# Two adapters and a mix on one Trainium2 core: the tile pipeline in two phases, and the mix as three products

## What is computed

```python
x = ...                       # 64 sequences x 32 rows x 512 features, fp32; the rows of one sequence share indices
# first block: a gated MLP, F = 1376, each of the three matrices with a rank-16 adapter chosen per sequence (16 adapters)
gate = x @ W_gate.T + 0.5 * (x @ A_gate[i].T) @ B_gate[i].T
up   = x @ W_up.T   + 0.5 * (x @ A_up[i].T)   @ B_up[i].T
act  = silu(gate) * up
h    = x + act @ W_down.T + 0.5 * (act @ A_down[i].T) @ B_down[i].T
# second block: the 32 rows of a sequence are mixed by one of 16 matrices of 32 x 32
out  = h + einsum('bct,bcd->bdt', h, weights[j])
```

## Time and profile before

| | us |
|---|---|
| three executions, median (lowest, highest) | 507.98 (503.09, 508.24) |
| the profiled execution, its own time | 507.72 |
| its span (first to last instruction) | 505.9 |
| PE busy in it | 480.2 (95%) |
| DVE / ACT / POOL busy | 237.8 / 159.4 / 118.6 |

### The profile page before, as it was taken

One profiled execution on the slowest core, in us unless ns is written; L12 is line 12 of the kernel. 1 busy time (PEld: TensorE's weight loads), 2 busy tenths in 40 slices (PEclk: granted clock), 3 DMA queues, 4 the chain that ended last, 5 costly groups with the idle time before them and its releaser, 6 DMA issues.

```text
span 505.9 us, 7251 instructions
## 1 busy us (share of the span) xinstructions
PE 480.2 (95%) x2716; PEld 430.2 (85%) x2716; DVE 237.8 (47%) x447; ACT 159.4 (32%) x244; POOL 118.6 (23%) x166
## 2 busy tenths in 40 slices
PE   2798599999999999999999999999999999999996
PEld 2677489899898989989898998989899898989985
DVE  2786525436353543635354362535536262553622
ACT  2764314232231424224142412414241241424120
POOL 5006040402305040220505022050502205050100
PEclk9799889999999999999999999999999999999998
DMA  7886151240604225060512406051240705123010
GB/s 246 325 263 228 60 200 48 64 180 1 223 21 171 73 74 171 1 223 21 171 73 78 167 1 224 19 183 62 87 157 2 230 12 195 50 92 132 1 41 21
DMA packets 16725, 58.13 MB, mean 115 GB/s; under 512 B 3184, under 2 KB 3696, under 8 KB 14672
## 3 DMA queue, kind: packets, MB, share of 16 engines
q0 software_dynamic: 5888, 36.97, 20.6%
q1 hardware_dynamic: 10832, 21.10, 12.9%
HBM read 53.86 MB, written 4.19 MB: 115 GB/s over the span
## 4 chain that ended last, share of the span: by engine, by line
PE 87%; DMA 4%; DVE 3%; POOL 3%; ACT 1%; issue 1%; SPq 0%; POOLq 0%; DVEq 0%
PE ps_down L673 26%; PE ps_gate L641 8%; PE ps_gate L643 8%; PE ps_gate L642 8%; PE ps_up L643 7%; PE ps_up L641 7%; PE ps_up L642 7%; PE ps_turn L662 4%; DMA b_raw<-in_b_rows,rows_now 3%; PE ps_misc L692 3%; POOL a_raw L322 3%; PE ps_gate L651 2%; PE ps_gate L650 2%; PE ps_up L650 2%; PE ps_up L651 2%; PE ps_down L683 2%
## 5 line engine op out<-in xcount | busy, mean ns | idle before, releaser
L446 DVE TENSOR_TENSOR actT_lo<-ps_turn,actT_hi 128x256 fp32r<-128x256 f32 (+1 forms) x64 | 32.0, 521 | 150.1 <-ACT actT_hi L346 115.4
L641 PE MATMUL ps_gate<-w_gate_hi,xT_hi 128*128 128x512 f32 (+3 forms) x196 | 77.8, 397 | 12.8 <-DVE w_gate_lo L446 12.8
L346 ACT ACTIVATE actT_hi<-ps_turn 128x256 fp32r<-128x256 f32 (+1 forms) x64 | 27.9, 461 | 165.6 <-PE ps_turn L662 162.1
L643 PE MATMUL ps_gate<-w_gate_hi,xT_lo 128*128 128x512 f32 (+3 forms) x196 | 77.3, 394 | 0.0
L642 PE MATMUL ps_gate<-w_gate_lo,xT_hi 128*128 128x512 f32 (+3 forms) x196 | 76.8, 392 | 0.0
L673 PE MATMUL ps_down<-wd_hi,actT_hi 128*128 128x288 f32 (+1 forms) x352 | 76.6, 299 | 0.0
L673 PE MATMUL ps_down<-wd_hi,actT_lo 128*128 128x288 f32 (+1 forms) x352 | 75.5, 295 | 0.0
L673 PE MATMUL ps_down<-wd_lo,actT_hi 128*128 128x288 f32 (+1 forms) x352 | 75.5, 296 | 0.0
L641 PE MATMUL ps_up<-w_up_hi,xT_hi 128*128 128x512 f32 (+1 forms) x192 | 74.1, 386 | 0.4 <-DVE w_up_lo L446 0.4
L331 POOL COPY mix_rows_now<-rows 128x1 int32 (+1 forms) x16 | 3.0, 187 | 300.4 <-DVE mix_w L509 300.4
L643 PE MATMUL ps_up<-w_up_hi,xT_lo 128*128 128x512 f32 (+1 forms) x192 | 71.3, 371 | 0.0
(11 more groups left out here) (66 smaller groups left out, 628.7 us busy)
## 6 DMA issues: line engine op xcount, KB each, us to landing
xT_raw<-in_xT SPq DMA_DIRECT2D x16, 256.0 KB, 2.6
x_sb<-in_x SPq DMA_DIRECT2D x16, 256.0 KB
out<-out_sb SPq DMA_DIRECT2D x15, 256.0 KB
landing<-in_w_down SPq DMA_DIRECT2D x5, 512.0 KB, 4.7
landing<-in_w_gate SPq DMA_DIRECT2D x4, 512.0 KB, 5.2
landing<-in_w_up SPq DMA_DIRECT2D x4, 512.0 KB, 4.8
a_raw<-in_a_rows,rows_now POOLq DMA_INDIRECT x64
landing<-in_w_gate SPq DMA_DIRECT2D x2, 352.0 KB, 3.8
```

What stands on the lines that cost most here:

```text
L346: return nc.scalar.activation(dst, src, ACT.Copy)
L446: return nc.vector.tensor_tensor(dst, src, hi_part.bitcast(F32), ALU.subtract)
L641: pe.matmul(ps[:, cols], x_hi, hi, start=(k == 0 and not columns), stop=False)
L643: last = pe.matmul(ps[:, cols], x_lo, hi, start=False, stop=stops and k == KH - 1)
```

## The change

The work is cut into two phases. **Phase 1** runs over 8 pairs of tiles and does gate and up only: six units per pair (three sections by two tiles), three PSUM banks each for gate and up instead of two, B rows gathered per section. A pair's eight sequences are dealt to its two tiles in an interleaved way. The activation isn't turned on PE: DVE transposes it in 32 x 32 blocks into `staging` (L679 of the changed kernel), and SP stores it to a DRAM tensor `actT_dram` that is already turned (`spill`, four DMAs per section and pair). **Phase 2** runs over 16 tiles: load `actT_dram`, split it, 66 down products, down adapter and mix of the tile before. Its POOL code is `gather_down`, its DVE code is the second `down`, its PE code the third. The SBUF of the gate and up weights is reused by the buffers of phase 2. The mix is three fp32r products of 512 columns: `mix_hi`, `mix_lo` by `h_hi`, `h_lo`, whose splitting is new work on ACT and DVE.

The core of the diff:

```diff
+                reached(ve, spilled[s], 64 * pr)
+                ve.wait_ge(act_ready, NU * pr + k + 1)
+                nc.vector.transpose(staging[s][:, :, t, :], act[k % 2][:, 0:n].rearrange("p (j c) -> p j c", c=BLOCK))\
+                    .then_inc(act_turned, 1)
...
+            def spill(pr, s):
+                c0, n = SECTIONS[s]
+                sp.wait_ge(act_turned, NU * pr + 2 * s + 2)
+                for q in range(TILE_SEQS):
+                    at = (q % 2) * 2 * BLOCK
+                    sp.dma_start(
+                        actT_dram[bass.ds(2 * pr + q // 2, 1), c0:c0 + n, at:at + 2 * BLOCK]
+                        .rearrange("o (j f) c -> f (o j) c", f=BLOCK),
+                        staging[s][q * BLOCK:(q + 1) * BLOCK, :, :, :].rearrange("f j t c -> f j (t c)"))\
...
+            def load_actT(m, e):
+                for s in range(NS):
+                    sp.wait_ge(spilled[s], 64 * (m // 2 + 1) if isinstance(m, int) else 64 * PAIRS)
+                reached(sp, actT_ready, m - 1)
+                sp.dma_start(
+                    actT_raw[e][:, 0:(NC - 1) * P].rearrange("p (c n) -> p c n", n=P),
+                    actT_dram[bass.ds(m, 1), 0:(NC - 1) * P, :].rearrange("o (c p) n -> p (o c) n", p=P))\
+                    .then_inc(actT_landed[e], 16)
...
+            def gather_down(m, first=False):
+                at = TILE_SEQS + 1
+                reached(pool, a_dn_ready, m)
+                pool.tensor_copy(a_dn_now[:, :], now(m)[:, at:at + TILE_SEQS]).then_inc(a_dn_now_copied, 1)
+                indirect_after(a_dn_now_copied, m + 1)
+                for q in range(TILE_SEQS):
+                    gather(a_dn_raw[:, q, :], a_dn_rows, a_dn_now[:, q:q + 1]).then_inc(a_dn_landed, 16)
+                reached(pool, mix_ready, m)
+                pool.tensor_copy(mix_now[:, :], now(m)[:, at + TILE_SEQS + 1:COLS]).then_inc(mix_now_copied, 1)
+                indirect_after(mix_now_copied, m + 1)
+                gather(mix_raw[:, :], mix_rows, mix_now[:, :]).then_inc(mix_landed, 16)
+                reached(pool, b_dn_ready, m)
+                pool.tensor_copy(b_dn_now[:, :], now(m)[:, at + TILE_SEQS:at + TILE_SEQS + 1])\
+                    .then_inc(b_dn_now_copied, 1)
+                if first:
+                    pool.wait_ge(xT_used[0], PAIRS)
+                    pool.wait_ge(xT_used[1], PAIRS)
+                indirect_after(b_dn_now_copied, m + 1)
+                gather(b_dn_raw[:, :], b_dn_rows, b_dn_now[:, :]).then_inc(b_dn_landed, 16)
...
-            def gathers(t, first=False):
-                if not first:
-                    pool.wait_ge(a_dn_ready, t)
-                    pool.wait_ge(b_dn_ready, t)
-                now = rows[:, bass.ds(t, 1), :].rearrange("p o c -> p (o c)")
-                pool.tensor_copy(rows_now[:, :], now[:, 0:TILE_SEQS + 1])\
...
+            def split_mix(m):
+                ve.wait_ge(mix_hi_ready, m + 1)
+                for q in range(TILE_SEQS):
+                    r = slice(q * CH, (q + 1) * CH)
+                    last = lo(mix_lo[r, r], mix_raw[r, :], mix_hi[r, r])
+                last.then_inc(mix_ready, 1)
...
+            def down(m, e, first=False, last=False):
+                if not first:
+                    mask_td(m - 1, 1 - e)
+                    split_mix(m - 1)
+                if not last:
+                    split_a_dn(m + 1, 1 - e)
+                if not first:
+                    residual_h(m - 1, 1 - e)
+                if not last:
+                    split_actT(m + 1, 1 - e)
+                split_b_dn(m)
+                if not first:
+                    residual_out(m - 1, 1 - e)
...
+            def pair(pr, final=False):
+                base(pr, 0)
+                lora(pr - 1, 5)
+                for k in range(1, NU):
+                    base(pr, k, final=final and k == NU - 1)
+                    lora(pr, k - 1)
...
-            def turn_act(t, s):
-                pe.wait_ge(act_ready, NS * t + s + 1)
...
+            def mix_products(out_, cols):
+                pe.matmul(out_, mix_hi[:, :], h_hi[:, cols], start=True, stop=False)
+                pe.matmul(out_, mix_lo[:, :], h_hi[:, cols], start=False, stop=False)
+                return pe.matmul(out_, mix_hi[:, :], h_lo[:, cols], start=False, stop=True)
+            def mix(m):
+                pe.wait_ge(mix_ready, m + 1)
+                pe.wait_ge(h_ready, 2 * m + 2)
+                mix_products(ps_mix[:, 0:H], slice(0, H)).then_inc(mix_done, 2)
...
+            def down(m, e, first=False):
+                pe.wait_ge(a_dn_ready, m + 1)
+                pe.wait_ge(actT_ready, m + 1)
+                reached(pe, h_ready, 2 * (m - 1))
+                down_chunks(m, e, 0, 3)
...
+                    down_lora(m - 1, 1 - e)
+                down_chunks(m, e, 3, 7)
...
+                    reached(pe, out_ready, m - 1)
+                    mix(m - 1)
...
+                down_chunks(m, e, 7, NC).then_inc(down_done, 1)
```

More of the change, by code:

```diff
@@ L42 @@
 TILES = SEQS // TILE_SEQS
+PAIRS = TILES // 2
 KH = H // P
 RR = TILE_SEQS * RANK
-SECTIONS = [(0, F - 1024), (F - 1024, 512), (F - 512, 512)]
+BLOCK = 32
+SECTIONS = [(0, 352), (352, 512), (864, 512)]
 NS = len(SECTIONS)
[L47 to L50, removed]
+UNITS = [(s, t) for s in range(NS) for t in range(2)]
@@ L51 @@
+NU = len(UNITS)
+TC = 2 * RR
+S0 = SECTIONS[0][1]
+W0 = TC + S0 + TC
+CHUNKS = [(c, min(P, F - c)) for c in range(0, F, P)]
 NC = len(CHUNKS)
-TC = 2 * RR
+LAST = CHUNKS[-1][1]
 A_GU = KH * 2 * RANK
[L54 to L72, removed]
@@ L75 @@
-PIECES = weight_pieces()
-GU_PIECES = sum(m != "down" for m, _, _ in PIECES)
-def pieces_to(m, s, k):
[L81 to L88, removed]
+A_DN = NC * RANK
+WD = RR + H + RR
+HALF = (RR + H) // 2
+PIECE = 512
+SLOTS = 5
+SETS = 3
+COLS = 2 * TILE_SEQS + 3
+PIECES = [(m, s, k) for s in range(NS) for m in ("gate", "up") for k in range(KH)]
@@ L285, in _ @@
[L285 to L292 removed]
+            load_xT(0, 0)
+            load_weights(0, KH)
+            sp.dma_start(low_rows[:, :], low).then_inc(low_landed, 16)
+            load_weights(KH, 2 * KH)
+            load_xT(0, 1)
+            load_weights(2 * KH, GU_PIECES)
@@ new lines, in _ @@
+            pair(0, first=True, weights=[(GU_PIECES, GU_PIECES + SLOTS)])
+            pair(1, weights=[(GU_PIECES + SLOTS, GU_PIECES + SLOTS + 3), (GU_PIECES + SLOTS + 3, len(PIECES))])
+            with sp.Fori(2, PAIRS - 1) as pr:
+                pair(pr)
+            pair(PAIRS - 1, last=True)
+            sp.wait_ge(w_ready, len(PIECES))
+            load_actT(0, 0)
+            spill(PAIRS - 1, 2)
+            sp.wait_ge(xT_used[0], PAIRS)
+            sp.wait_ge(xT_used[1], PAIRS)
+            load_x(0, 0)
@@ L338, in _, with indirect_after, now, gather @@
-            gathers(0, first=True)
-            with pool.Fori(1, TILES) as t:
-                gathers(t)
+            def indirect_after(semaphore, value, cell=0):
+                pool.wait_ge(semaphore, value)
+                pool.tensor_tensor(waited[:, cell:cell + 1], lane_sb[0:1, 0:1], lane_sb[0:1, 0:1], ALU.add)
+            def now(tile):
+                return rows[:, bass.ds(tile, 1), :].rearrange("p o c -> p (o c)")
+            def gather(dst, src, offsets):
+                return pool.indirect_dma_start(dst, None, src, bass.IndirectOffsetOnAxis(ap=offsets, axis=0))
@@ L610, in _ @@
             ve.wait_ge(mask_ready, 1)
[L611 to L625 removed]
+            split_x(0, 0)
@@ new lines, in _ @@
+            split_a_dn(0, 0)
+            split_actT(0, 0)
+            gating(PAIRS - 1, 5)
+            ve.wait_ge(xT_used[0], PAIRS)
+            ve.wait_ge(xT_used[1], PAIRS)
+            down(0, 0, first=True)
+            down(1, 1)
+            down(2, 0)
+            down(3, 1)
+            with ve.Fori(2, TILES // 2 - 1) as j:
+                down(2 * j, 0)
+                down(2 * j + 1, 1)
+            down(TILES - 2, 0)
+            down(TILES - 1, 1, last=True)
+            m, e = TILES - 1, 1
```

1099 lines of the change are left out of this document (637 added, 462 removed).

## The result

The changed kernel takes **676.81 us** (median of 4 runs, 676.41 to 677.47) against 508.11 us for the kernel before in the same session (4 runs, 503.09 to 509.37): 1.335 times as long, with an interval of 1.326 to 1.344. The forecast was 684 us. The profiled execution took 677.47 us for a span of 675.7 us.

The account below looks back on a forecast made before the run. PE was to bound phase 1 until 311 us, then a loop of waits at 24.2 us a tile: 311 + 353 + 11 + 7.5 = 682 us of span, forecast 684 us. The 8-in-10 range was 630 to 728 us.

Parts of the forecast that it names:

- PE's work and phase 1: Gate and up phase: PE sets 36.1 us a pair, DVE's transposes and POOL's gathers hidden; phase ends at T = 311 us.
- Phase 2 closes a loop: Down phase: waits through POOL, ACT, DVE and PE make 24.2 us a tile where PE has 10 us of work.
- (a): After the last down product of tile k−1: adapter product masked, turned and split, mix split; `mix_ready` at 2.6 us.
- (b): POOL, only after `mix_ready`: mix gather, B rows of tile k, A rows of tile k+1; 9.8 us with hops.
- (c): Landing of the last gather, from the end of its issue to the split that waits for it: 1.9 us.
- (d): ACT's and DVE's split of the A rows: 0.78 and 0.88 us, done at 16.0 us of the step.
- (e): `residual_h` behind the A split on DVE (0.75 us), then h split on ACT and DVE; done at 17.7 us.
- (f): PE waits 11.6 us at the mix, then mix and 24 products take 6.4 us at a lowered clock, plus a hop.
- The clock costs less: Rival, chance 0.18: PE keeps full clock in phase 2, mix and 24 products 3.9 us, loop 21.7 us, 652 us.
- The spill fills the DMA engines: Rival, chance 0.09: phase 1's short-run stores cost 33 us a pair by packets, pairs take 44 us; 739 us.
- PE stays the bound: Rival, chance 0.07: POOL's gathers run a tile ahead, phase 2 loop is PE's 10.0 us; 484 us, 5% faster.
- The mix gains nothing: Rival, no separate chance: three products behind a wait cost as much as one fp32 product, a 2.7 us difference.

Follow-up runs that it names:

- run 1: Changed kernel, with POOL gathering the A rows of tile k+1 ahead of the B and mix rows of tile k: 530.6 us.
- run 4: Changed kernel plus 66 products into an unused PSUM bank ahead of PE's wait at the mix, results unused: 661.46 us.
- run 8: Changed kernel with every spill stored twice, the second time to a DRAM array that nobody reads: 684.6 us.
- run 5: run 1 plus the residual and the split of h ahead of the A split on DVE and ACT: 526.19 us.
- run 7: run 5 with two buffers for the A rows of down instead of one: 510.32 us.
- run 9: run 7 with SP issuing each activation load half a turn (one tile) earlier, ahead of an output store: 500.07 us.
- run 11: run 9 with the mix as one fp32 product, without the splits of h and mix rows: 498.96 us.
- run 3: Changed kernel with the mix as one fp32 product, without the splits of mix and h, order unchanged: 655.63 us.
- run 10: run 5, with one buffer of A rows, plus the activation load issued half a turn earlier: 515.48 us.

## Why the prediction was right

**PE's work and phase 1.** Right. Two `b_now` copies of POOL one pair apart start at 203.89 and 240.29: 36.4 us, forecast 36.1. That neither DVE's transposes nor POOL's 14 gathers bind shows in PE's 252.00 of 252.00 us. The start was mis-sized: phase 1 ends at T = 316.9 instead of 311.

**Phase 2 closes a loop.** Right, and shown by taking it apart: run 1 undoes the named order of POOL and the step falls from 22.8 to 12.4 us, both by `t_dn`. Part by part, against the forecast from the last down product (452.19), in the step shown:

| part | forecast | measured |
|---|---|---|
| (a) to `mix_lo` done | 2.6 | 454.87 − 452.19 = 2.7 |
| (b) POOL, six gathers | 9.8 | 463.68 − 454.87 = 8.8 |
| (c) landing | 1.9 | 465.25 − 463.68 = 1.6 |
| (d) A split | 1.7 | 466.96 − 465.25 = 1.7 |
| (e) residual, h | 1.7 | 468.65 − 466.96 = 1.7 |
| (f) mix and 24 products | 6.5 | 474.12 − 468.65 = 5.5 |

(b) is the term that was too large. Six tenths of its 1 us are the mix gather: the earlier trace rows priced its group at 2.31 us, with a gather of 1.56 us that ran beside DVE's `wd_lo` and `b_dn` (first line, the kernel before); here it takes 0.98 with DVE idle, and the group 1.7. The group of the B rows needs 1.6 us instead of 1.77 and the four gathers 5.4 instead of 5.54:

```profile
241.04 1.56 POOL L333 DMA_INDIRECT mix_raw<-in_mix_rows,mix_rows_now  x1 [0.27 <-issue]
...
455.01 0.18 POOL L413 COPY mix_now<-rows 128x1 int32 x1 [14.53 <-DVE mix_lo L621]
...
455.73 0.98 POOL L374 DMA_INDIRECT mix_raw<-in_mix_rows,mix_now  x1 [0.28 <-issue]
...
458.32 0.19 POOL L408 COPY a_dn_now<-rows 128x4 int32 x1
...
462.73 0.95 POOL L374 DMA_INDIRECT landing<-in_a_dn_rows,a_dn_now  x1 [0.30 <-issue]
```

(f) was right in the mean: 6.28 us over the 14 steps, against 6.4 and a hop. It is 5.5 in the step shown because the low clock ended after 2.9 us there; in the step of 513.41 (last line) it held for 5.9, and in the 14 steps it ran from 2.9 to 6.0 us, around the 5.2 of the earlier trace rows:

```profile
458.20:468.60 10.40, 0.01 (x1) 0.00 (x0) 2.32 (x5) 2.03 (x4) 4.32 (x7) 0.65 0.21 60
468.60:471.50 2.90, 2.85 (x9) 2.57 (x10) 2.02 (x3) 1.36 (x3) 0.00 (x0) 0.50 0.00 0
471.50:474.10 2.60, 2.60 (x22) 2.60 (x21) 0.93 (x2) 0.00 (x0) 0.00 (x0) 0.99 0.24 86
...
513.40:518.40 5.00, 4.99 (x18) 4.72 (x19) 2.95 (x4) 1.32 (x3) 0.00 (x0) 0.50 0.03 11
```

In the next step 0.50 holds for 4.9 us and the step is 22.80 long; the shortest steps are 21.9, the longest 23.55. What the low clock adds, 6.28 − 4.18 = 2.1 us a step by run 4's undisturbed tiles, was put at 2.5.

**The sum** holds better than its terms, which is partly luck: a late start and shorter loops make up for each other. Forecast span: 311 + 14 to the start of step 1, 14 × 24.2 = 339, 18.5 behind it, 682. Measured: 336.97 to the start of step 1, 319.8 for the 14 steps, 18.9 behind it, 675.7. Step 1 begins 12 us late: 5.9 of it is the start of the run, and 1.1 the first product of `down(0)`, at T + 5.1 instead of T + 4. The other 5 us are a path that the forecast didn't have: the way of tile 1's activation through DRAM. PE had just waited, so the first 6.4 us of `down(0)` ran at a clock of 0.51, and yet its last product ends at 333.7, before it matters. `t_dn` stands on DVE behind the split of the second activation: its last section is turned at 323.3 and spilled, its load is issued at 326.1 and lands at 333.2, the split waits 5.38 us for it and, with that of the B rows behind it, holds `t_dn` until 336.97. These 12 us take back more than half of the 19 us by which the 14 loops are shorter.

**The rivals.** *The clock costs less*: no. (f) is 6.28 us in the mean, near the forecast's 6.5 and far from the rival's 3.9. Its price of the clock, 32 us, was not far off: run 4 keeps the full clock and its 14 steps gain 26 us. The prediction let DVE's work end at 21.9 us and bound the loop there; by an estimate from run 4 it would end at 20.3, for there an undisturbed step is 20.68 us, with DVE idle for the last 0.40 of it. *The spill fills the DMA engines*: refuted by run 8. Its cost can be read off: 0.308 × 16 × 682.1 − 0.238 × 16 × 675.7 = 788 us of engine time for eight pairs' second spill, 6.2 us a pair on 16 engines, beside my 4 by bytes and 33 by packets. That is an upper bound, since packets also slow one another: the same 12800 packets of POOL's queue took 0.190 × 16 × 682.1 − 0.185 × 16 × 675.7 = 73 us more in run 8. The second bound was off because it carried the 96 ns of a packet of 1948 bytes over to one of 256: here it is 788 us for 45568 more packets, at most 17 ns each.

By the rule that the prediction took from the Trainium skill, *DMA: Bandwidth & Descriptors*, Specifications, a run below 512 bytes costs a read and a write of its surroundings. The measured 6.2 us a pair lies between one and two times the 4 us by bytes, so short stores seem to cost more than their bytes, in that direction, though part of the 2 us can be the slowing of other packets; it decided nothing here, since the DMA engines stood idle for 0.47 of the phase.

*PE stays the bound*: decided at the place named for it, whether the A rows are gathered before `mix_lo` of the tile before. But the prediction had the other half wrong. It said that POOL one tile ahead was enough for 484 us; run 1 gave 530.6. Behind the order stood three more things: the A split ahead of the residual (4 us in run 5, little beside the spread of the runs), one buffer of A rows (16 us in run 7), and a load queued behind a store (10 us in run 9). With all four changed PE's 10.0 us a tile comes true, 10.00 undisturbed and 10.10 in the mean; no run leaves the A split alone in its old place, so that it is needed isn't shown. Run 9 is still 16 us above the rival's 484, 10 of them because step 1 begins at 334.9 instead of T + 14 = 325. *The mix gains nothing*: this rival was right in effect, and the forecast's sentence that the new mix saves 2.7 us whatever else happens was wrong. At PE's bound the three products take 0.12 us a tile less, but the time is the same within the measurement (500.07 against 498.96, run 11); in the kernel as changed it costs 21 us net (run 3), because its splits stand ahead of POOL's gathers and behind the residual.

## What to carry to other kernels

When a change leaves an engine less work per step, walk once round every single buffer: who frees it, what stands in program order between that and the next fill, how long the landing takes; the longest round is the new step, whatever the busy shares say. An in-order queue that issues transfers (POOL's gathers, SP's loads) should have first what is needed last in the chain, and never wait for a result of the step that its own transfers feed. Expect loops to be nested: after each fix look for the wait that ends last now, and stop only where the bound engine shows none.

## What the runs showed of the hardware

- The first of four gathers (418.55 to 420.41) took 1.86 us of POOL beside DVE's `actT_lo` (to 419.75) and `b_dn`; the second, beside `out_sb` and `t_dn`, took 0.95 like the two after it (run 5). With DVE idle all four took 0.95 to 0.99 (the kernel after). Why some DVE operations go with a long gather and others don't isn't shown.
- The split of gathered rows began 1.6 us after the end of the last issue in the kernel after (DMA share 0.19 meanwhile), 4.07 and 3.37 us after it on average in runs 5 and 10, where the load of an activation ran beside it (share 1.00 and 1.02 in one landing each), and 1.89 us after it in run 10's last tile, which has no such load (0.43).
- PE's granted clock was 0.50, 1.2 of 2.4 GHz, for 2.9 to 6.0 us of work after each wait of some 10 us, against 5.2 us at tile 1 of the kernel before. Sixty-six idle products brought it back to 1.00 and took 26 us out of 14 steps, 8 of which they cost again in the last tile. The cure of the wait bought 146.
- The fp32 product of 512 columns is only 0.12 us dearer on TensorE than three fp32r products of them: those take 423.23 − 422.50 = 0.73 us in run 9, so the one costs 0.85, next to the 0.86 of the earlier trace rows.
